# Decoder block: cross-attention spread over more steps, its scores from high and low parts, and GpSimd's arithmetic on VectorE

## The reference, cut to what matters

```python
x = x + self_attention(layernorm(x))                       # 16 heads of 32, ALiBi, rational softmax
x = x + cross_attention(layernorm(x), ctx, mask)           # 8 heads of 64, context of 750 x 384
x = x + moe_ffn(layernorm(x))                              # 8 experts, top 2, capacity 896

# cross_attention
q = (x @ W_q);  k = (context @ W_k);  v = (context @ W_v)  # per head 64 wide
sim = einsum('bihd,bjhd->bhij', q, k) * 64 ** -0.5
sim = where(mask[:, None, None, :], sim, max_neg)
out = einsum('bhij,bjhd->bihd', softmax(sim), v) @ W_o + b_o
```

## Time and profile before

| | |
|---|---|
| runs | 3488.24, 3491.22, 3494.34 us; median 3491.22 |
| profiled execution | 3495.34 us, span 3493.6 us |
| cross-attention in it | weights from 767 us, first product 796.8, last slot written 2084 |
| busy, whole span | PE 89%, PEld 72%, DVE 48%, ACT 40%, POOL 21% |

### The profile page before, as it was taken

One profiled execution on the slowest core, in us unless ns is written; L12 is line 12 of the kernel. 1 busy time (PEld: TensorE's weight loads), 2 busy tenths in 40 slices (PEclk: granted clock), 3 DMA queues, 4 the chain that ended last, 5 costly groups with the idle time before them and its releaser, 6 DMA issues. The chain is left out here.

```text
span 3493.6 us, 52659 instructions
## 1 busy us (share of the span) xinstructions
PE 3107.0 (89%) x19340; PEld 2532.3 (72%) x19340; DVE 1690.5 (48%) x3672; ACT 1403.8 (40%) x2345; POOL 726.0 (21%) x564
## 2 busy tenths in 40 slices
PE   5888898958989988999999957999999999999997
PEld 4667777746777767777777735888788878888886
DVE  5888888843555555555555532333233322323232
ACT  5777777624555555555555521111111111111111
POOL 0000000001111121111111113242424242423343
PEclk9899999978999999999999977999999999999999
DMA  2111111122111111111111002131313131313132
GB/s 92 32 37 46 42 42 42 45 68 100 36 41 35 35 45 54 35 35 35 35 41 35 16 27 102 49 97 55 87 53 91 49 91 49 101 53 89 55 85 58
DMA packets 96194, 193.83 MB, mean 55 GB/s; under 512 B 18656, under 2 KB 28640, under 8 KB 94016
## 3 DMA queue, kind: packets, MB, share of 16 engines
q1 hardware_dynamic: 80912, 160.78, 14.9%
q0 software_dynamic: 15152, 31.26, 4.2%
HBM read 144.19 MB, written 47.82 MB: 55 GB/s over the span
## 5 line engine op out<-in xcount | busy, mean ns | idle before, releaser
L1612 DVE CAST f_hh<-f_hf 128x448 fp32r<-128x448 f32 x256 | 116.9, 457 | 891.7 <-ACT f_hf L1636 859.1
L1636 ACT ACTIVATE f_hf<-f_h 128x448 f32<-128x448 f32 x256 | 139.6, 545 | 1015.8 <-PE f_h L1672 987.6
L1688 PE MATMUL f_y<-f_w2h,f_hh 128*128 128x512 f32 x896 | 357.9, 399 | 0.0
L1559 POOL TENSOR_TENSOR f_w1l<-f_raw,f_w1h 128x512 fp32r<-128x512 f32 x130 | 183.4, 1411 | 828.5 <-DVE f_w1h L1594 828.3
L1688 PE MATMUL f_y<-f_w2h,f_hl 128*128 128x512 f32 x896 | 354.1, 395 | 0.0
L1688 PE MATMUL f_y<-f_w2l,f_hh 128*128 128x512 f32 x896 | 352.3, 393 | 0.0
L1247 ACT COPY c_pT<-c_psum 125x672 f32<-125x672 f32 x256 | 184.2, 719 | 311.7 <-PE c_psum L1353 309.9
L1255 ACT ACTIVATE c_s_sb<-c_s_sb,c_nmx 112x750 f32<-112x750 f32 x256 | 236.0, 922 | 161.9 <-DVE c_nmx L1091 159.0
L1672 PE MATMUL f_h<-f_xTh,f_w1h 128*128 128x448 f32 x1024 | 262.2, 378 | 32.5 <-ACT f_hf L1636 16.8
L1353 PEld LDWEIGHTS c_psum<-c_ident,c_s_sb 112*125 112x125 f32 x1536 | 204.1, 198 | 84.4 <-issue 78.1
L1672 PE MATMUL f_h<-f_xTl,f_w1h 128*128 128x448 f32 x1024 | 256.0, 372 | 0.0
(11 more groups left out here) (243 smaller groups left out, 5970.0 us busy)
## 6 DMA issues: line engine op xcount, KB each, us to landing
f_raw<-in_w SPq DMA_DIRECT2D x132, 512.0 KB
c_craw<-in_ctxT SPq DMA_DIRECT2D x16, 1125.0 KB, 5.5
a_x_in<-in_x SPq DMA_DIRECT2D x9, 896.0 KB, 5.6
a_xr<-in_x SPq DMA_DIRECT2D x8, 896.0 KB, 5.9
x_dram<-a_xr SPq DMA_DIRECT2D x8, 896.0 KB, 4.8
q_dram<-a_q SPq DMA_DIRECT2D x32, 224.0 KB, 5.3
c_q<-q_dram SPq DMA_DIRECT2D x16, 448.0 KB, 5.2
c_x<-x_dram SPq DMA_DIRECT2D x16, 448.0 KB, 5.6
```

The costliest lines, as they stand in the source:

```text
L1559: pool.tensor_tensor(w1s[1][:, n % NSLOT].rearrange("p k c -> p (k c)"), raw1[:, g % 2, n % 2, :], w1s[0][:, n % NSLOT].rearrange("p k c - ...
L1612: dve.tensor_copy(hs[0][:, l % 2, c * HC:c * HC + HC], hf[:, c, :]).then_inc(h_hi, 1)
L1636: act.activation(hf[:, c, :], H[:, 0:HC], ACT.Gelu_apprx_tanh).then_inc(free, 1)
L1688: mm = pe.matmul(Y[t][:], hs[a][:, l % 2, 128 * t:128 * t + 128], w2s[b][:, l % NSLOT, :], start=j == 0 and q == 0, stop=j == FB - 1 and q ...
```

## The change

- Scores are the sum of three products of fp32r parts: high queries x high keys, high x low, low x high. So keys and queries have two parts each. ScalarE makes the high parts where it made copies before; VectorE subtracts for the low parts, and a K bank is free only after that subtraction.
- The context's low parts and both bias additions move from GpSimd to VectorE. GpSimd keeps the table stores.
- The plan puts the units in other steps and another order. The tail's work moves to later steps. Only the middle and last slots are used.
- `s_sb` holds eight heads (NS = 8); VectorE masks an odd head ahead of the normalising and no longer waits for old transposes.
- ScalarE makes the next context's high parts one per step in steps 4 to 6, and at step 6 waits for OUT(1) ahead of its PV(0) copy.

The diff, cut (semaphore declarations and the removed GpSimd code, which is in the listing above, are left out):

```diff
-        kT = sb("kT", [128, NM, J])
+        kT = [sb(f"kT{k}", [128, NM, J], F32R) for k in "hl"]
         v = sb("v", [JB, NJ, C])
         q2 = sb("q2", [128, KC, T])
-        q = sb("q", [128, KC, T])
+        q = [sb(f"q{k}", [128, KC, T], F32R) for k in "hl"]
         m8 = sb("m8", [R, J], U8)
         mb = sb("mb", [R, J])
-        s_sb = sb("s_sb", [R, 4, J])
+        NS = 8
+        s_sb = sb("s_sb", [R, NS, J])
         mx, nmx, den, rec = (sb(n, [R, NH]) for n in ("mx", "nmx", "den", "rec"))
...
-        PLAN = {0: ([], [K(3, 1)], []), 1: ([], [PV(3)], [V(1, 0)]), 2: ([], [V(1, 1)], []), 3: ([], [V(1, 2), OUT(0)], []),
-                4: ([], [OUT(1)], []), 5: ([], [PV(0)], []), 6: ([], [XT(0)], []), 7: ([K(0, 0)], [K(0, 1)], [XT(1)]),
-                8: ([], [K(1, 0)], []), 9: ([], [PV(1)], [RT]), 10: ([], [V(0, 0)], []), 11: ([K(1, 1)], [K(2, 0)], []),
-                12: ([], [V(0, 1)], []), 13: ([], [PV(2)], [PRE]), 14: ([], [V(0, 2)], []), 15: ([K(2, 1)], [K(3, 0)], [])}
+        PLAN = {0: ([], [K(3, 1)], []), 1: ([], [PV(3)], [V(1, 0)]), 2: ([], [V(1, 1)], []), 3: ([], [V(1, 2)], []),
+                4: ([], [OUT(0)], []), 5: ([], [PV(0)], []), 6: ([], [OUT(1)], []), 7: ([], [K(0, 0)], [K(0, 1)]),
+                8: ([], [K(1, 0)], []), 9: ([], [PV(1)], [XT(0)]), 10: ([], [XT(1)], [K(1, 1)]), 11: ([], [V(0, 0)], [K(2, 0)]),
+                12: ([], [RT], []), 13: ([], [PV(2)], [V(0, 1)]), 14: ([], [K(2, 1)], []), 15: ([], [PRE], [V(0, 2), K(3, 0)])}
         LATE = (K(3, 1), V(1, 0), V(1, 1), V(1, 2))
-        START = [K(0, 0), K(0, 1), K(1, 0), K(1, 1), K(2, 0), V(0, 0), V(0, 1), V(0, 2), K(2, 1), K(3, 0)]
+        START = [K(0, 0), K(0, 1), K(1, 0), K(1, 1), V(0, 0), K(2, 0), V(0, 1), K(2, 1), V(0, 2), K(3, 0)]
...
             what, m, a = unit
             if what == "K":
-                return kT[:, m, K0[a]:K0[a] + KW[a]], bank(kind, unit)[:, 0:KW[a]]
+                return lambda part: kT[part][:, m, K0[a]:K0[a] + KW[a]], bank(kind, unit)[:, 0:KW[a]]
...
+            def send(i):
+
                 wait_apart(pool, slots_made, i)
                 for q in range(4):
                     pool.indirect_dma_start(out=table_dram, out_offset=bass.IndirectOffsetOnAxis(ap=slotu[:, q:q + 1], axis=0),
                                             in_=pay[:, q, :], in_offset=None, bounds_check=E * CAP - 1, oob_is_err=False).then_inc(sent, 16)
 
...
+            with pool.Fori(1, B + 1) as i:
+                send(i)
...
+            def lo_of_context(i, k):
+                dve.wait_ge(c_hi, i * CC + k + 1)
+                dve.tensor_tensor(cT[1][:, k, :], craw[:, k, :], cT[0][:, k, :].bitcast(F32), ALU.subtract).then_inc(c_lo, 1)
+
+            def add_bias(i):
+                dve.wait_ge(x_loaded, i * 16 + 16)
+                dve.tensor_tensor(x1[:], x1[:], bo[:, None, :].broadcast_to([R, 2, C]), ALU.add).then_inc(x1b_made, 1)
+
+            def with_bias(i):
+                dve.wait_ge(out_stored, i * 16 - 16)
+                dve.tensor_tensor(xo[:], x1[:], bi[:, None, :].broadcast_to([R, 2, C]), ALU.add).then_inc(xo_made, 1)
...
 
-                dve.wait_ge(s_full, i * (NH // 2) + h // 2 + 1)
-                if h % 2 and not (isinstance(i, int) and i * NH + h - 3 <= 0):
-                    dve.wait_ge(pt_full, i * NH + h - 3)
+                if h % 2 == 0:
+                    dve.wait_ge(s_full, i * (NH // 2) + h // 2 + 1)
...
+            def lo_of_queries(i, g):
+                dve.wait_ge(q_hi, i * 2 + g + 1)
+                dve.tensor_tensor(q[1][:, 2 * g:2 * g + 2], q2[:, 2 * g:2 * g + 2], q[0][:, 2 * g:2 * g + 2].bitcast(F32), ALU.subtract).then_inc(q_made, 1)
+
+            def lo_of_keys(i, kind, unit):
+                dve.wait_ge(gen_hi, number(SPLIT, i, kind, unit) + 1)
+                dst, src = unit_places(kind, unit)
+                dve.tensor_tensor(dst(1), src, dst(0).bitcast(F32), ALU.subtract).then_inc(gen_free[BANK[kind, unit]], 1)
...
-                if s in (3, 4):
-                    residual(i, kind, s - 3)
-                elif s == 5:
+                if s in (5, 7):
+                    residual(i, kind, s // 7)
+                elif s == 8:
                     layernorm(i)
-                elif s == 10:
+                elif s == 9:
+                    with_bias(i)
+                elif s == 13:
                     routing(i, kind, 0)
-                elif s == 14:
+                elif s == 14 and kind != "end":
+                    add_bias(i)
+                elif s == 15:
                     routing(i, kind, 1)
...
+            for k in range(CC):
+                lo_of_context(0, k)
+            add_bias(0)
+            for g in range(2):
+                lo_of_queries(0, g)
+            for unit in START:
+                if unit[0] == "K":
+                    lo_of_keys(0, "start", unit)
...
-                    if s in (6, 10, 14):
+                    if s in (7, 10, 14):
                         lo_of_outputs(i, kind, (s - 6) // 4)
                     elif s == 2 and kind != "first":
                         lo_of_outputs(i - 1, kind, NM - 1)
+                    if s % 2 and has_step(kind, s + 2):
+                        masked(*step(i, s + 2))
                     if has_step(kind, s + 2):
...
-                    if has_step(kind, s + 2):
+                    if s % 2 == 0 and has_step(kind, s + 2):
                         masked(*step(i, s + 2))
+                    if s in (5, 6, 7) and kind != "last":
+                        lo_of_context(i + 1, s - 5)
+                    for unit in (projections(kind, s - 1, (1, 2)) if s else []):
+                        if unit[0] == "K":
+                            lo_of_keys(i, kind, unit)
+                    if s in (8, 15) and kind != "last":
+                        lo_of_queries(i + 1, s // 9)
                     if kind != "first":
                         tail(i, kind, s)
+                if kind != "last":
+                    lo_of_keys(i, kind, K(3, 0))
...
+                if unit[0] == "K":
+                    act.copy(dst(0), src).then_inc(gen_hi, 1)
+                else:
+                    act.copy(dst, src).then_inc(gen_free[BANK[kind, unit]], 1)
...
-                if s == 4:
+                if s == 7:
                     act.wait_ge(mv_made, i * 2)
                     act.activation(rstd[:], mv[:, :, 1], ACT.Abs_reciprocal_sqrt, bias=eps[:]).then_inc(root_made, 1)
-                elif s in (7, 8):
-                    unit = XT(s - 7)
+                elif s in (10, 11):
+                    unit = XT(s - 10)
                     act.wait_ge(gen_full, number(ORDER, i, kind, unit) + 1)
-                    act.copy(xnT[:, s - 7, :], bank(kind, unit)[:, 0:KC * R]).then_inc(gen_free[BANK[kind, unit]], 1)
-                elif s == 10:
+                    act.copy(xnT[:, s - 10, :], bank(kind, unit)[:, 0:KC * R]).then_inc(gen_free[BANK[kind, unit]], 1)
+                elif s == 13:
                     act.wait_ge(gen_free[BANK[kind, RT]], uses_before(i, kind, RT) + 1)
                     act.activation(lg[:], lg[:], ACT.Exp).then_inc(le_made, 1)
...
+                    if s in (4, 5, 6) and kind != "last":
+                        if s == 4:
+                            act.wait_ge(gen_full, number(ORDER, i, kind, V(1, 2)) + 1)
+                        hi_of_context(i + 1, s - 4)
+                    if s in (6, 9, 13):
+                        if s == 6 and kind != "first":
+
+                            act.wait_ge(gen_full, number(ORDER, i, kind, OUT(1)) + 1)
                         hi_of_outputs(i, kind, (s - 5) // 4)
...
-                for a in range(2):
-                    for e in range(2):
-                        rows = slice(64 * e, 64 * e + 64)
-                        j0 = a * (J - HW)
-                        mm = pe.matmul(scb[e][0:R, a, 0:HW], q[rows, m, t0:t0 + R], kT[rows, m, j0:j0 + HW],
-                                       start=True, stop=True, tile_position=(64 * e, 0))
+                for x, y in ((0, 0), (0, 1), (1, 0)):
+                    for a in range(2):
+                        for e in range(2):
+                            rows = slice(64 * e, 64 * e + 64)
+                            j0 = a * (J - HW)
+                            mm = pe.matmul(scb[e][0:R, a, 0:HW], q[x][rows, m, t0:t0 + R], kT[y][rows, m, j0:j0 + HW],
+                                           start=(x, y) == (0, 0), stop=(x, y) == (1, 0), tile_position=(64 * e, 0))
...
-                        made_before(i, kind, 3)
+                        made_before(i, kind, 2)
...
-            made(0, "start", K(1, 0))
             made(0, "start", K(1, 1))
+            made(0, "start", K(2, 1))
...
-                        if s == 6:
-                            made_before(i, kind, 2)
-                        elif s == 10:
+                        if s == 10:
                             made(i, kind, K(3, 1))
                         elif s == 14:
```

(57 more changed lines are left out.)

15 lines of the change are left out of this document (7 added, 8 removed).

## The result

The changed kernel takes 3590.7 us, the median of four runs from 3589.03 to 3595.11. The kernel before takes 3492.4 us beside it, four runs from 3488.24 to 3494.34. The ratio is 1.0285, with a 95% interval of 1.0272 to 1.0298. So the sign of the forecast holds and its range too, but the loss is 98 us where 51 were worked out.

What follows compares the result with a forecast made beforehand. TensorE's work, its waits and the slow clock were taken to bound it: 68 - 2.4 + 13 + 4 = 82.6 us a body, +56 over 14 bodies, +51 with start and end, so 3542 us; range 3474 to 3610.

Steps and rivals of the forecast that it cites:

- the term for the slow clock: Middle bodies: TensorE at 1.2 GHz after waits costs 4 us a body (ends 0 and 8), against 3 before.
- Scores: Score units in the middle bodies: 1.15 us each with overlapping row tiles, 2.4 us a body saved.
- the second rival: Score units: the two fp32r tiles do not overlap, 0.9 us more per unit, 3650 us; chance 0.12.
- VectorE: Middle bodies: VectorE's work rises from 43.2 to about 50 us a body, well under the period.
- The waits: Middle bodies: TensorE waits 13 us a body, in six places plus 0.5 elsewhere, where it waited 7.3.
- The one for K(0,1) in step 7: Step 7: K(0,1) waits 1.7 us for OUT(1)'s bank, behind ScalarE's copy and VectorE's queue.
- The walk: One middle body followed through the new plan: six places stop TensorE, for 13 us with 0.5 elsewhere.
- Start and end: Outside the middle bodies: start -1 us, first body 0, last body -4.
- My 0 for the first body: First body: the K waits and the lighter scores cancel, 0 us.
- The rival "gains stay, the clock stays high": Middle bodies: new waits leave the clock at 2.4 GHz, 3458 up to 3486 us; chance 0.17.
- Its own point of decision: Middle bodies: the sign turns on whether waits and clock together cost under 13 us a body, against 10.3 before.

Runs made afterwards that it cites:

- e4: Kernel before, with idle TensorE products filling its three waits of about 2 us: 3468.2 us, ratio 0.9932.
- e5: Changed kernel with idle TensorE products in its six waits, the last placed ahead of the wait for its bank: 3523.47 us, ratio 1.0085.
- e6: Changed kernel with ScalarE's and VectorE's parts of the next context one step earlier: 3544.37 us, ratio 1.0147.
- e1: Changed kernel with plain float32 scores back, keys and queries in one part, all else as changed: 3524.9 us, ratio 1.0082.
- e7: Changed kernel with float32 scores and idle TensorE products in its three waits: 3454.26 us, ratio 0.9889.
- e2: Kernel before with only the scores from high and low parts, old plan, GpSimd keeping its work: 3538.09 us, ratio 1.013.
- e12: Changed kernel, high and low parts kept, with the context one step earlier and ScalarE's XT(0) and XT(1) copies earlier: 3435.05 us, ratio 0.9841.
- e11: Changed kernel with float32 scores, the context one step earlier and ScalarE's XT(0) and XT(1) copies earlier: 3348.06 us, ratio 0.9593.
- e8: Kernel before with GpSimd's context subtractions and bias additions on VectorE, old plan and float32 scores: 3492.04 us, ratio 0.9993.
- e10: Changed kernel with the context's low parts and both bias additions back on GpSimd: 3534.17 us, ratio 1.0118.
- e9: Kernel before with ScalarE's copy of XT(0) moved ahead of the exponential, to the head of step 7: 3430.76 us, ratio 0.9827.

## Why the prediction was right, and where it was not

The sign and the kind of loss were right, its size was not: the term for the slow clock was too small. Per middle body, the change of 7.5 us comes apart by `e4` and `e5`, in which both kernels run at full clock:

| | before | after | measured | forecast |
|---|---|---|---|---|
| work and waits, period with fills | 77.0 | 80.8 | +3.8 | 78.6 - 75.3 = +3.3 |
| slow clock, net | 1.5 | 5.3 | +3.7 | 4 - 3 = +1 |

The fills run past their waits by some 0.5 us before and 1.8 us after, so up to 1.3 us may belong in the second row and not in the first. The timelines as they ran agree: work 1.9 us less (forecast 2.4), waits 5.1 more (5.7), slow clock some 4 more (1).

- *Scores*, 1.15 us a unit: 1.21, so 1.9 us a body saved and not 2.4. The two fp32r tiles overlap, and the second rival (3650) falls. The rule of the Trainium skill (TensorE: Matmul & The Clock Gate, Part 3) by which the unit would take 1.5 us isn't borne out here: 0.3 us less. (By it the unit would have cost 8 x 0.35 = 2.8 us a body more than my sum, and not 2.6.)
- *VectorE*, 50 us a body: 48.9. Its own amount of work is hidden, as said.
- *The waits*, 13 us: 12.4. Five of the six are where they were put and within 0.7 us (1.61, 1.76, 1.40, 2.14, 2.59 for 1.7, 1.8, 2.1, 2.4, 2.8). The one for K(0,1) in step 7 isn't there. In its place K(0,0) waits 2.90 us. The walk let K(0,0) wait for its bank only; it waits also for the context's third low part, which the change put behind a mask and a normalising in VectorE's step 7. The sum came out nearly right by luck: the missed wait stands in the predicted one's place, and `e6` shows what is left for K(0,1) without it, 0.46 us.
- *The slow clock*, 4 us: this is the term that was mis-sized. The step is "I take one slow stretch like today's plus part of another, less what the waits absorb". The changed kernel has three to four stretches a body, 7.1 us gross and 5.3 net (`e5`), and by the mean clocks of 0.90 and 0.95 about 17 us a body stand at 1.2 GHz where 8 stood before; and I had booked the kernel before at its gross 3 where `e4` shows 1.5 net. A difference of 1 us became 3.7: 2.7 x 14 = 38 us of the 49 that the middle bodies lack (105 - 56). Work and waits (0.5) and the rounding of the before column (78.3 against 78.6, 0.3) are the rest. `e1` shows the same by itself: waits of nearly the same sum as before, at other places, make the body 3.5 us longer, and `e7` shows that the difference goes when the clock stays up (76.56 against 77.0). I let the price follow the number of today's stretches. It hangs also on what stands behind the wait: one stretch of `e1` costs 2.6 us, nearly as much as all those of a body before (some 3).
- *Start and end*: -5 forecast, -11 measured, and the two parts were both wrong, in opposite directions. The first product comes 4.4 us earlier (796.79 to 792.37), but from there to step 0 of body 1 it takes 94.9 us and not 85.0: TensorE waits there 3.72 us for a mask and 4.45 for the context's low part, where it waited 1.78 and 1.87, and 1.57 and 1.33 for low key parts. My 0 for the first body left these out. So the start costs 5.5 us where I gave -1. From step 0 of body 15 to the experts' first product it takes 112.2 us and not 126.2: -13.9 where I gave -4. There TensorE waits 1.07 and 0.19 us for masking, where it waited 2.30 and 4.62, and the clock in the stage's end is 0.87 against 0.82; what each is worth is not separated. The experts' part is 2.7 us shorter, which also differs by up to 5 us between runs that leave it alone.
- *The rival "gains stay, the clock stays high"* falls: the clock is 0.90. Its own point of decision, waits and clock under 13 us a body together, was right: they came to 12.4 + 7.1, and the kernel got slower.

The parts are not additive. High and low parts cost 3.0 us a body in the old plan (`e2`), 4.1 in the new one as it ran (`e1`) and 80.8 - 76.6 = 4.2 at full clock (`e5`, `e7`), 5.5 where no other wait is left (`e12`, `e11`). Moving GpSimd's arithmetic to VectorE costs 0 in the old plan (`e8`) and 4.2 in the new (`e10`). Not separated: the biases' move from the context's, since `e10` takes both, and the new plan by itself from `NS = 8`. Fills on `e12` were not tried.

## What to carry to other kernels

When a unit moves, list every semaphore that it waits for, not its bank alone, and put what frees a bank or completes an operand ahead of long work in its engine's queue: two such moves of copies and subtractions took 177 us off here (`e1` to `e11`), while moving work from one engine to another in the old plan took nothing (`e8`). Count a wait of TensorE at its length plus what the slow clock takes from the products behind it, which can be as much again and more: in `e1` two K units behind a wait of 2.9 us lost 2.6 us more, and a V unit with most of a K unit behind one of 2.1 us lost 2.7. A kernel with idle products in its waits shows in one run how much of a period is clock, at least, as far as the products don't outlast the waits.

## What the runs showed of the hardware

- The price of waits is not their length. 7.3 us cost at least 1.5 us of clock a body (`e4`), 7.7 us in three other waits at least 5.5 (`e7`), 12.4 us in six waits at least 5.3 (`e5`); the excess of the slow groups is some 3, 6.3 and 7.1. Length alone does not decide: in the kernel before, 1.96 to 1.98 us ahead of a score unit left it at 1.45 us to the next start in 13 of 14 bodies, and in `e9` the same wait left it at 1.8 to 2.5 us in three of 14. What does decide stays open.
- Twelve fp32r matmuls with 64 rows each, in two row tiles, take 1.21 us in all, 0.10 a record; eight float32 records of the same shapes take 1.45, 0.18 each.
- A subtraction of 750 columns takes 1.78 us on GpSimd (`e10`, the median of 48) and 0.93 on VectorE, a bias addition of 1024 columns 2.35 to 2.41 and 1.22. Where GpSimd's share overlaps a multiply of VectorE, that one takes 1.68 us in the earlier trace rows and 0.76 to 0.97 in a body of `e10`, and 0.61 otherwise; taking all of it away (`e8`) still changed no time, since another wait took its place. The Trainium skill (SBUF — State Buffer, SBUF: two separate sides) has an exclusive pair of ports that GpSimd shares with VectorE instructions in a two-port mode or with two SBUF inputs: the one that starts first keeps it for its whole instruction. The long multiply fits that; no run here shows which mode it was in.
